# Attention probabilities of two tasks in one buffer, one transposing DMA and one store per pair, all loads issued by SyncE, four buffers of x

## What is computed

```python
x = x + 0.5 * ffn(layernorm(x))          # pass A of a batch row
x = x + attention(layernorm(x))          # 16 heads of width 8
x = x + 0.5 * ffn(layernorm(x))          # pass B of a batch row

def ffn(x):                              # 8 experts, F = 512, all summed
    for wg, wu, wd in experts: acc += (silu(x @ wg) * (x @ wu)) @ wd

def attention(x):                        # q, k with rotary embedding; rel = clipped relative positions
    scores = q @ k.T + q . rel           # causal
    attn = softmax(scores)
    return (attn @ v + attn . rel) @ w_o.T
```

## Time and profile before

| | us |
|---|---|
| three executions | 1436.86, 1435.93, 1439.6 (median 1436.86) |
| profiled execution, its own time | 1438.3 |
| its span, first to last instruction | 1436.5 |
| around the span | 1.8 |
| PE busy | 1375.4 (96%) |
| DVE busy | 1278.3 (89%) |
| ACT busy | 1101.9 (77%) |
| POOL busy | 1087.4 (76%) |

### The profile page before, as it was taken

How to read it: one execution, slowest core, us unless ns; L and a number is a source line. 1 busy time by engine, 2 the same in 40 slices (tenths; PEclk the granted TensorE clock), 3 DMA queues, 4 the chain that set the end, 5 groups by cost and what they waited for, 6 DMA issues and landing times.

```text
span 1436.5 us, 29572 instructions
## 1 busy us (share of the span) xinstructions
PE 1375.4 (96%) x8632; PEld 1076.9 (75%) x8632; DVE 1278.3 (89%) x2541; ACT 1101.9 (77%) x2642; POOL 1087.4 (76%) x956
## 2 busy tenths in 40 slices
PE   8999999999999999999999999999999999999898
PEld 7787676777777777777777778777777777778686
DVE  6887898999999999999999989899999999899565
ACT  6656778878778887788888878778887778788454
POOL 7967787787778877887778768787777877677555
PEclk9999999999999999999999999999999999999999
DMA  6404999999999999999999999899999999897200
GB/s 185 142 15 125 154 192 187 178 204 170 180 188 175 165 178 176 187 160 189 164 152 209 170 167 179 148 191 177 171 172 161 192 162 173 161 173 142 44 1 8
DMA packets 718386, 225.08 MB, mean 157 GB/s; under 512 B 652305, under 2 KB 697745, under 8 KB 718225
## 3 DMA queue, kind: packets, MB, share of 16 engines
q1 hardware_dynamic: 556224, 172.45, 72.9%
q10 hardware_dynamic: 162000, 50.75, 19.4%
HBM read 60.95 MB, written 69.86 MB: 91 GB/s over the span
## 4 chain that ended last, share of the span: by engine, by line
PE 47%; DVE 19%; ACT 9%; issue 7%; DMA 6%; ACTq 4%; SPq 4%; POOL 3%; POOLq 0%; DVEq 0%
PE work L708 9%; PE work L710 9%; PE work L709 9%; PE acc L786 5%; PE acc L787 4%; DVE hid L1071 4%; PE acc L791 4%; DMA probs_t<-probs 4%; DVE hid L1065 3%; DVE negmax L1167 3%; ACTq L1000 3%; PE work L839 3%; DVE work L1162 3%; ACT work L960 2%; DVE probs L1176 2%
## 5 line engine op out<-in xcount | busy, mean ns | idle before, releaser
L1218 POOL TENSOR_TENSOR hid_lo<-hid,hid_hi 128x512 fp32r<-128x512 f32 x512 | 663.5, 1302 | 215.6 <-ACT hid_hi L915 115.1
L909 ACT ACTIVATE hid<-work 128x512 f32<-128x512 f32 x512 | 310.1, 606 | 123.9 <-PE work L710 84.9
L1065 DVE SCALAR_TENSOR_TENSOR hid<-hid,work 128x512 f32<-128x512 f32 x512 | 345.7, 680 | 53.9 <-ACT hid L909 53.4
L1071 DVE TENSOR_TENSOR hid<-hid,work 128x512 f32<-128x512 f32 x512 | 346.6, 680 | 33.6 <-PE work L710 31.2
L915 ACT CAST hid_hi<-hid 128x512 fp32r<-128x512 f32 x512 | 320.1, 630 | 49.7 <-DVE hid L1071 30.8
L786 PE MATMUL acc<-hid_hi,wd 128*128 128x512 f32 x512 | 216.5, 423 | 12.4 <-ACT hid_hi L915 9.9
L1167 DVE TENSOR_REDUCE negmax<-work 128x1 f32<-128x384 f32 (+3 forms) x352 | 219.2, 634 | 1.2
L1233 POOL TENSOR_TENSOR probs<-exps,probs 128x512 f16<-128x512 f32 (+1 forms) x160 | 172.0, 1075 | 62.8 <-ACT probs L972 59.8
L708 PE MATMUL work<-xt,wg 128*128 128x512 f32 x512 | 207.0, 404 | 5.4 <-DVE xt L1040 1.5
L708 PE MATMUL work<-xt,wu 128*128 128x512 f32 x512 | 206.1, 402 | 2.8 <-DVE hid L1071 1.9
L791 PE MATMUL acc<-hid_lo,wd 128*128 128x512 f32 x512 | 204.1, 401 | 1.0 <-POOL hid_lo L1218 0.7
(11 more groups left out here) (97 smaller groups left out, 2184.5 us busy)
## 6 DMA issues: line engine op xcount, KB each, us to landing
prob_window_scratch<-probs SPq DMA_DIRECT2D x384, 80.0 KB, 3.5
rel_win<-rel_window_scratch ACTq DMA_DIRECT2D x250, 96.0 KB, 4.3
q_scratch<-rope SPq DMA_DIRECT2D x16, 512.0 KB, 4.2
qq<-q_scratch ACTq DMA_DIRECT2D x32, 256.0 KB
rel_window_scratch<-g_s SPq DMA_DIRECT2D x32, 256.0 KB, 5.1
k_scratch<-rope SPq DMA_DIRECT2D x16, 512.0 KB, 4.2
kk<-k_scratch ACTq DMA_DIRECT2D x32, 256.0 KB
prob_window_scratch<-probs SPq DMA_DIRECT2D x32, 256.0 KB, 3.2
```

What stands on the lines that cost most here:

```text
L909: act.activation(hid[:, arg % HB, :], work[bank_of["gate", arg]][:, :], ACT.Tanh, scale=0.5).then_inc(s_tanh, 1)
L1065: dve.scalar_tensor_tensor(out=hid[:, arg % HB, :], in0=hid[:, arg % HB, :], scalar=1.0, in1=work[bank_of["gate", arg]][:, :], op0=ALU.add ...
L1071: dve.tensor_tensor(hid[:, arg % HB, :], hid[:, arg % HB, :], work[bank_of["up", arg]][:, :], ALU.mult).then_inc(s_hid, 1)
L1218: pool.tensor_tensor(hid_lo[:, arg % 2, :], hid[:, arg % HB, :], hid_hi[:, arg % 2, :].bitcast(F32), ALU.subtract).then_inc(s_hlo, 1)
```

## The change

- `XB` is 4 and `PASSES` has another order: B0 and B1 follow each other, as do A4 and A5, B2 and B3, A6 and A7.
- Two tasks form a pair (the single task of tile 0 stays alone), 6 pairs in a group and 192 in all. `probs` has 3 places of a pair, `probs_t` 3 places of a pair. One `p_turn` of up to 16 blocks and one `store_band` serve a pair; both wait for both tasks' low halves. `p_hi` waits for an earlier pair only at the first task of a pair.
- `load_q`, `load_k`, `load_window` and `load_band` are issued by SP.
- The scores of tile 0 are one matmul of 512 columns, with q as the weights and four masked copies of k as the moving side. So `q_pad` of tile 0 reads `kk` and waits for `load_k`.
- `v_s` moves into a half of `rope`, which adds waits: `project` of a batch row waits for the last `v_split` of the row before, `v_add` for the stored k.
- The planner has new numbers: another `LATER`, the attention's first two batch rows due in 144 units each (157.5 before) and the other six in 162.7, `ln_scaled` with 1.54 in place of 0.7, no extra for a matmul after short ones.

```diff
-    XB = 5
+    XB = 4
-    TB = 6
-    PB = 4
+    TB = 3
+    PB = 3
-    PASSES = (("A", 0), ("A", 1), ("A", 2), ("A", 3), ("B", 0), ("A", 4), ("B", 1), ("A", 5), ("B", 2),
-              ("A", 6), ("B", 3), ("A", 7), ("B", 4), ("B", 5), ("B", 6), ("B", 7))
+    PASSES = (("A", 0), ("A", 1), ("A", 2), ("A", 3), ("B", 0), ("B", 1), ("A", 4), ("A", 5), ("B", 2),
+              ("B", 3), ("A", 6), ("A", 7), ("B", 4), ("B", 5), ("B", 6), ("B", 7))
...
+    FAST = 144
...
+        done = k // NK + sum(weight[:k % NK]) / sum(weight)
+        rest = (UNITS_TO - UNITS_FROM - 2 * FAST) / (B - 2)
+        due.append(UNITS_FROM + FAST * min(done, 2) + rest * max(done - 2, 0))
...
+    def pair_of(k):
+        return k // GK * GP + (k % GK + 1) // 2
...
-        step("ACT", 0.7, time, "ln_scaled", what, ("ln_shift", what))
+        step("ACT", 1.54, time, "ln_scaled", what, ("ln_shift", what))
...
-                step("ACT", 0.55, max(begin - 13, first - 13), "load_window", quad, ("qrel_store", gg),
+                step("SP", 0.95, max(begin - 13, first - 13), "load_window", quad, ("qrel_store", gg),
...
-            step("SP", 1.5 if columns == L else 1.25, due[k] + 2, "p_turn", k, lower(k),
-                 ("values", values_of(quad_of(k - TB)) if k >= TB else None), ("split_lo", (E - 1, 2)), lands=LATE)
+        for m in range(GP * HG * t, GP * HG * (t + 1)):
+            k = pair(m)[-1]
+            done = [lower(x) for x in pair(m)]
+            step("SP", 1.6, due[k] + 2, "p_turn", m, *done,
+                 ("values", values_of(quad_of(pair(m - TB)[-1])) if m >= TB else None), ("split_lo", (E - 1, 2)), lands=LATE)
...
-        probs = sb("probs", [P, PB, 2 * L], F16)
-        probs_t = sb("probs_t", [P, TB, L])
+        probs = sb("probs", [P, PB, 4 * L], F16)
+        probs_t = sb("probs_t", [P, TB, 2 * L])
...
-                    for n, a in enumerate(places):
-                        done = pe.matmul(bank[:, n * keys:(n + 1) * keys], q_pad[:, quad % 2, a, :],
-                                         kk[:, gg % 2, 0:keys], start=True, stop=True)
+                    if i == 0:
+                        pe.wait_ge(s_qld[gg % 2], 16 * (gg // 2 + 1))
+                        done = pe.matmul(bank[:, :], qq[:, gg % 2, 0:P], q_pad[:, quad % 2, :, :].rearrange(
+                            "p a k -> p (a k)"), start=True, stop=True)
...
-                    if arg >= PB:
-                        act.wait_ge(*turned(arg - PB))
-                        act.wait_ge(*stored(arg - PB))
+                    m = pair_of(arg)
+                    if arg == pair(m)[0] and m >= PB:
+                        act.wait_ge(*turned(m - PB))
+                        act.wait_ge(*stored(m - PB))
```

267 lines of the change are left out of this document (136 added, 131 removed).

## The result

The changed kernel takes 1439.97 us (median of 20 runs, 1437.82 to 1444.2), the kernel before in the same comparison 1435.64 (20 runs, 1430.18 to 1440.0). The ratio is **1.0034, 95% interval 1.0024 to 1.0045**: slower by 0.3%, where 1.2% faster was forecast (1420 us, in a range of 1398 to 1446 that also took in a part of the rivals' cases; the forecast's own case was 1406 to 1432). A second comparison gave 1443.91 against 1433.20 us: 1.0070 (1.0041 to 1.0098). So the changed kernel is slower by 0.3 to 0.7%, and where a later run is set against it both ratios are used. The profiled execution has a span of 1438.3 us.

The account below looks back on a forecast made before the run. PE, busy 1375.4 of 1436.5 us, was taken as the bound, with DVE next. Gains of 6 + 7 + 6.5 + 8 = 27.5 us less 9 lost took 1438.3 to 1419.8, rounded to 1420 us, range 1398 to 1446.

Parts of the forecast that it names:

- What SP gets: Sync engine's list: loses 160 turns (205 us) and 224 stores, gains 238 us of loads, gets no longer; taken as nothing.
- Scores: Scores of tile 0 on PE: one matmul of 512 columns for four of 128, 32 times; 6 us gained.
- Layer norm: PE's waits for the layer norm's scaled rows shrink with the planner's right cost; 7 us gained, bounds 0 and 9.2.
- Places: Places for the probabilities: ACT's wait for a turn and the clock drop behind it go; 6.5 us gained, bounds 0 and 9.3.
- Loads off ACT: ACT loses all its DMA issues, so its waits behind them go; 8 us gained, bounds 0 and 17.
- (a): Turns of pairs land about 1.9 us later, so PE waits more for turned probabilities; 4 us lost, bounds 0 and 115.
- (b): `q_pad` of tile 0 stands between `load_k` and the first scores, 32 times; 1 us lost, bounds 0 and 33.
- (c): Loads wait in SP's list behind turns, so `near` on DVE waits for windows; 3 us lost.
- the first rival: Windows come late behind transposes on SP's queue, holding `near` on DVE; 1463 us, from 1441 on, chance 0.16.
- (d): First two batch rows at 144 units each raise DVE's 93% to some 96%; 1 us lost, between 0 and 12.
- (e): `project` waits for `v_split` and `v_add` for the stored k, eight times each; nothing, or 8 x 1.3 = 10 us.
- the gains are refilled: Rival: PE's waits on ACT vanish, but turns and `values` take their place; 1439 us, 1433 to 1441, chance 0.11.

## Why the prediction was wrong

**The step that failed is "What SP gets".** It priced the sync engine's list at nothing: "With the stores its list gets no longer", and "SP waited for its inputs for 146 us in one group alone, so even most of the upper bound is covered". Both halves were wrong. First, the list got 107 us longer (867 to 974). The loads took 304 us and not 238, and 160 turns fewer saved 75 us and not 205. The bounds for a turn (1.28 to 2.56 us) did hold in the sum: 192 turns took 479 us, 233 more than at 1.28 each, of the 246 that were the upper bound; single wide places have medians of 3.6 and 4.1. It was the price that was missing. Second, idle time in an in-order list is no cover. In the changed kernel the sync engine still pauses for 165 us; those pauses are at moments of their own, and at others a band turn stands behind 5 us of issues. The runs with cut stores and with the bands on ScalarE measured the price from both sides: some 60 us of issuing more (979 to 1038, in one comparison) cost 20 us, 77 us less (974 to 897) won 12 to 18. So each us issued at that fullness is worth some 0.16 to 0.35 us of time, and the 107 us that the change added to 867, by this estimate, 17 to 37. Within that lie the 23 us between the forecast's 18.5 gained and the 4.9 lost (0.34% of 1436).

That the step failed is shown; that it accounts for all of the 23 us is not. With the list back at the fullness of the kernel before (q, k and bands on ScalarE, 0.71) PE still waited 11.1 us for the two, against 5.7, and the time was 0.9970; the best of these runs has 0.9947, where the forecast was 1.2% less. Some 10 us of the shortfall are left open. And whether the list's time or the load of the DMA engines behind it is the scarce thing, no run separates. That 1440 lies inside the stated range is no merit of the sum: the range was drawn wide enough to hold a part of the rivals. One sign of being wrong that the prediction named, a list of the sync engine that is full, is close to what happened.

**Scores** (6): right as a size, 18.9 became 13.1 us of PE; the run that undid it gives none or about 2 of the 5.1 back in time.

**Layer norm** (7): right. The 14 waits of 9.2 us in all are gone, and so is the one of 3.68 us that stood under places; only the tail's is left, as named, and it grew from 2.76 to 3.8 us. Net of the 3.68 that is 8.1 us.

**Places** (6.5): half. ACT's wait for a turn is gone. But the granted clock was to be 1.00 until the tail, and the run's mean fell from 0.994 to 0.980: the term counted the drop that was avoided and none of those behind new waits.

**Loads off ACT** (8, bounds 0 to 17): mechanism right, and in the changed kernel's order the size far too small. The waits behind issues went from 54.1 to 3.8, and undoing the move costs 35 to 40 us; it comes from the windows, which alone cost some 50, while the other loads do no harm on ScalarE. I had half of three groups of waits as the upper bound; undone, all waits behind issues together are 45.7 us, and the time is nearly their full sum longer. What the move alone won in the order of the kernel before no run shows, since there it filled the sync engine's list.

**(a) turns** (4): 8.6 us more of waits, within the bounds. That turns land later than before is not shown: the median from issue is 4.5 us where it was 4.6. It hides two places with medians of 6.0 and 6.5 us, near the 6 to 7 forecast for wide turns, but the turns of the same tasks had medians of 3.7 to 7.2 in the kernel before. What is new is the time that a turn spends in the list ahead of its issue. The band turns, 8.3 us more of waits, were in no term; they stand in the same list. The DMA engines were no fuller for it, their share in the stretch fell from 1.06 to 0.93. **(b)** `q_pad`: PE waits 1.1 us for it, as taken. **(c)** and the first rival, windows late: false. DVE shows no wait for `rel_win`, and a window lands 2.7 us after its issue where it took 4.3 (what it waits in the list ahead of its issue is not in either). **(d)** the fast rows: DVE is at 1123.58 of 1207.4 us, 93% as before, and the table with the faster pace shows no cost. **(e)** nothing, as taken.

The rule of the Trainium skill ("DMA: Bandwidth & Descriptors", "Queues, rings and completion order") on which I built that rival would have the windows behind the transposes; by that rule, worked out as I did it, they would land later, and the trace, counted from the issue, shows them earlier. That need not refute the rule: the turns' issues hold the list, so the issue of a window does not begin while a turn ahead of it is still being issued. The other rule of the page ("Issuing engines are not separate DMA queues"), that issuing from several engines saves the issuing engine's time alone, names what this case came to: the issuing engine's time, 0.81 of the stretch, was what the forecast priced at nothing. Here the trace agrees with the rule in the main and not to the letter, since with the loads of the changed kernel back on ScalarE a window lands in 4.2 us and not 2.7. I had taken from the rule that the move costs the transfers nothing, and overlooked the issuing engine's own time.

As a check, PE's starts over the run, each against the typical distance of its kind, give this rough ledger from before to after: work at its pace 1303.1 to 1295.0 us, slower pace without a wait shown 56.3 to 40.5, waits 61.9 to 76.4, lower clock outside waits 7.4 to 18.3. The first two are gains, 24 us, near the 27.5 that I forecast. The last two, 25 us, took them back. Of the rivals "the gains are refilled" describes it, with chance 0.11 and a price of 21 us for terms (a) to (d); the refill came from a term that was not among them.

## What to carry to other kernels

Before moving DMA issues to another engine, sum the issue times of that engine's list and divide by the stretch: here 0.72 went with 5.7 us of waits, 0.81 with 22.6 and most of a gain of over 20 us lost, and 0.90 lost 80. Idle time of an in-order issuing engine is not cover; a list that mixes transposes with small loads delays what stands behind them. Move only the issues that hurt where they are (here the windows), and leave the others (here the bands) where a short issue meets an engine that has room. And look at the medians place by place: here one median hid turns of 1.4 and of 4.1 us.

## What the runs showed of the hardware that I had not expected

- The issue of a transposing DMA held the sync engine for 1.4 to 1.5 us (median by place in the group) at 8 and 12 blocks, 2.4 to 4.1 at 16, from 1.49 us at least to 6.75 at most, with all its inputs ready. Cut into halves of 8 the same blocks took no less (512 us of issuing for 479).
- The same 192 turns took 437 us to issue where stores were cut in two and 562 where the windows carried 16.4 MB more: the same transposes do not cost the same issue time; it depends on what else is under way, by the second run on the bytes that the DMA engines move beside them.
- A window load landed in 2.7 us from its issue when it shared the sync engine's queue with the turns, in 4.3 on ScalarE's own queue.
- Behind PE waits of 2.25 to 3.21 us the granted clock was 0.57 over 12 us, part of it at 1.2 in place of 2.4 GHz; with PE busy through the same waits it was 1.00, and the whole time, six waits filled, 0.2 or 0.6% less.
